# Cross-attention with a new order inside its steps: maxima, scores, maxima, weighting, values, keys

## What is computed

```python
q1 = x1 @ Wq1                      # x1 = layernorm(x), 8 heads of 64
k  = concatenate([x1 @ Wk1, x2 @ Wk2], axis=1)   # x2 = context, 256 + 4096 keys
v  = concatenate([x1 @ Wv1, x2 @ Wv2], axis=1)
sim  = einsum('bihd,bjhd->bhij', q1, k) * scale
attn = softmax(sim, axis=-1)
out  = einsum('bhij,bjhd->bihd', attn, v) @ Wo + bo
```

## Time and profile before

| | us |
|---|---|
| three runs | 1909.60, 1912.25, 1913.94 (median 1912.25) |
| the profiled execution, its own time | 1913.26 |
| its span, first to last instruction | 1911.5 |
| PE busy | 1654.2 (87%) |
| DVE busy | 1221.1 (64%) |
| ACT busy | 727.5 (38%) |
| POOL busy | 424.3 (22%) |

### The profile page before, as it was taken

How to read it: one execution, slowest core, us unless ns; L and a number is a source line. 1 busy time by engine, 2 the same in 40 slices (tenths; PEclk the granted TensorE clock), 3 DMA queues, 4 the chain that set the end, 5 groups by cost and what they waited for, 6 DMA issues and landing times. The chain is left out here.

```text
span 1911.5 us, 30641 instructions
## 1 busy us (share of the span) xinstructions
PE 1654.2 (87%) x12438; PEld 1266.1 (66%) x12438; DVE 1221.1 (64%) x1434; ACT 727.5 (38%) x970; POOL 424.3 (22%) x254
## 2 busy tenths in 40 slices
PE   5999989999989999989999997287357776999999
PEld 4777767777767777767777775165133334788888
DVE  4686586586586576586576585634579994644444
ACT  3444354344354334344334333122353331334332
POOL 4200041000041000041000000110056661445552
PEclk9999999999999999999999999597579998799999
DMA  4000120000120000120000000100000001111100
GB/s 151 12 18 1 45 73 1 12 18 1 37 81 1 12 18 1 35 81 4 12 10 10 1 1 4 54 1 0 15 0 1 1 0 34 67 56 44 55 11 23
DMA packets 43357, 47.89 MB, mean 25 GB/s; under 512 B 5200, under 2 KB 30672, under 8 KB 43232
## 3 DMA queue, kind: packets, MB, share of 16 engines
q1 hardware_dynamic: 43232, 46.07, 7.8%
HBM read 45.02 MB, written 1.05 MB: 24 GB/s over the span
## 5 line engine op out<-in xcount | busy, mean ns | idle before, releaser
L493 DVE TENSOR_REDUCE xa_maxes<-psum 128x2 f32<-128x1024 f32 (+1 forms) x288 | 332.5, 1162 | 267.3 <-PE psum L674 267.3
L419 ACT ACTIVATE xa_probs<-psum 128x1024 f32<-128x1024 f32 x272 | 269.0, 1026 | 323.9 <-PE psum L707 311.1
L514 DVE TENSOR_TENSOR xa_prob_sum<-xa_prob_sum,xa_probs 128x1024 f32<-128x1024 f32 x240 | 308.9, 1287 | 11.2 <-ACT xa_probs L419 10.4
L719 PE MATMUL psum<-xa_probs,xa_vals 128*64 128x256 f32 x2176 | 263.1, 385 | 2.1 <-DVE xa_heads_T L528 1.6
L719 PEld LDWEIGHTS psum<-xa_probs,xa_vals 128*64 128x64 f32 x2176 | 146.5, 136 | 93.0 <-issue 23.9
L344 POOL TENSOR_TENSOR xa_w_lo<-xa_stage,xa_w_hi 128x768 fp32r<-128x768 f32 x16 | 31.9, 1994 | 617.0 <-ACT xa_w_hi L379 617.0
L606 PE MATMUL psum<-xa_wv_hi,xa_ctx_hi 128*128 128x256 f32 x512 | 148.9, 291 | 21.3 <-DVE xa_maxes L493 18.6
L701 PE MATMUL psum<-xa_q_hi,xa_k_hi 64*128 64x256 f32 x1088 | 156.5, 284 | 0.6 <-issue 0.6
L705 PE MATMUL psum<-xa_q_hi,xa_k_lo 64*128 64x256 f32 x1088 | 154.6, 280 | 0.0
L707 PE MATMUL psum<-xa_neg_max,xa_ones 64*128 64x256 f32 x1088 | 154.5, 280 | 0.0
L703 PE MATMUL psum<-xa_q_lo,xa_k_hi 64*128 64x256 f32 x1088 | 154.0, 279 | 0.0
(11 more groups left out here) (273 smaller groups left out, 3482.8 us busy)
## 6 DMA issues: line engine op xcount, KB each, us to landing
xa_ctx_in<-in_ctxT_dram SPq DMA_DIRECT2D x32, 512.0 KB, 3.7
xa_stage<-in_L_xattn_Wk_dram SPq DMA_DIRECT2D x32, 128.0 KB, 2.3
xa_stage<-in_L_xattn_Wv_dram SPq DMA_DIRECT2D x16, 256.0 KB, 3.0
ex_raw<-in_L_ffn_w_gate_dram SPq DMA_DIRECT2D x8, 512.0 KB, 3.6
ex_raw<-in_L_ffn_w_up_dram SPq DMA_DIRECT2D x8, 512.0 KB, 4.5
ex_raw<-in_L_ffn_w_down_dram SPq DMA_DIRECT2D x8, 512.0 KB, 3.5
xa_stage<-in_L_xattn_Wq_dram SPq DMA_DIRECT2D x16, 128.0 KB, 2.3
X<-in_x_dram SPq DMA_DIRECT2D x1, 1024.0 KB, 5.4
```

The lines of the kernel that those rows point to most:

```text
L419: nc.scalar.activation(probs[:, n % RING, :], S[:, 2 * (n % 2):2 * (n % 2) + 2, :].rearrange("p h q -> p (h q)"), ACT.Exp, scale=HD ** -0. ...
L493: dve.tensor_reduce(maxes[:, qt, :, g:g + 1], max_banks(v, g, qt)[:, :, 0:group_keys(g)[1]], AX_X, ALU.max).then_inc(max_reduced, 1)
L514: dve.tensor_tensor(prob_sum[:, :], prob_sum[:, :], probs[:, n % RING, :], ALU.add).then_inc(summed, 1)
L719: i = pe.matmul(O[half[h], 0:N1], vals[:, 2 * j + t, lanes:lanes + HD], probs[:, n % RING, (2 * h + t) * N1:(2 * h + t + 1) * N1], start=( ...
```

## The change

In a step PE does the weighting directly behind the first half of the maxima, then the values, then (in step 2 of some units) the output projection, then the keys. ACT's queue follows: it stores the values before the high part of the keys. In the last step PE scores the second half of the maxima before the first, which `turn` tells DVE, and turns the maxima before the values; the second tile of values waits there until DVE has read the turned maxima. Sums of a unit are inverted and applied at the end of DVE's step 0, no longer in step 1. DVE's queue in a step becomes reduction of (d - 1, tile 1), low part of the keys of group d, a sum, reduction of (d, tile 0), a sum. No instruction is added or taken away.

```diff
+        def turn(v, g, qt):
+            return 1 - qt if v > 0 and g == NG - 1 else qt
@@ ScalarE
+                for c, j in v_due(u, d):
+                    store_values(c, j)
                 if d + 1 < NG and v < U:
                     store_k_hi(v, d + 1)
-                for c, j in v_due(u, d):
-                    store_values(c, j)
@@ VectorE
             def reduce_max(v, g, qt):
-                dve.wait_ge(max_scored, (v * NG + g) * QT + qt + 1)
+                dve.wait_ge(max_scored, (v * NG + g) * QT + turn(v, g, qt) + 1)
...
                         reduce_max(v, 0, 0)
-                        split_keys(v, 1)
-                    add_probs(u, 1)
+                    if u > 0:
+                        invert_sums(u - 1)
+                        normalize(u - 1)
                     continue
                 if v < U:
                     reduce_max(v, d - 1, 1)
-                if d == 1 and u > 0:
-                    invert_sums(u - 1)
-                    normalize(u - 1)
-                if d >= 2 and not (d == STEPS - 1 and v < U):
-                    add_probs(u, 2 * d - 1)
-                if v < U:
-                    reduce_max(v, d, 0)
-                if d == 2 and u > 0 and u % PAIRS == 0:
-                    add_output(u // PAIRS - 1)
+                    if d < STEPS - 1:
+                        split_keys(v, d)
+                    else:
+                        reduce_max(v, d, 1)
+                        reduce_max(v, d, 0)
+                        reduce_rows(v)
+                        split_keys(v, d)
+                        store_neg_max(v)
+                add_probs(u, 2 * d - 1)
                 if d < STEPS - 1:
+                    if v < U:
+                        reduce_max(v, d, 0)
+                    if d == 2 and u > 0 and u % PAIRS == 0:
+                        add_output(u // PAIRS - 1)
                     add_probs(u, 2 * d)
-                    if v < U:
-                        split_keys(v, d + 1)
                     if d == 4 and u % PAIRS == 2 and u + 2 < U:
                         split_own(u // PAIRS + 1)
-                elif v < U:
-                    reduce_max(v, d, 1)
-                    reduce_rows(v)
-                    add_probs(u, 2 * d - 1)
-                    store_neg_max(v)
@@ TensorE
                 if following:
-                    score_for_max(v, d, 0, values)
-                    maxima = (v * NG + d) * QT + 1
                     if d == STEPS - 1:
                         score_for_max(v, d, 1, values)
-                    if d == 2 and u > 0 and u % PAIRS == 0:
-                        project_output(u // PAIRS - 1)
-                    if d + 1 < NG:
-                        project_keys(v, d + 1, maxima, values)
-                    for c, j in v_due(u, d):
-                        project_values(c, j, maxima)
-                        values += 1
+                    score_for_max(v, d, 0, values)
+                    maxima = (v * NG + d) * QT + (2 if d == STEPS - 1 else 1)
                 if d == 0 and u > 0:
                     sum_probs(u - 1)
                 for j in step_tiles(d - 1):
                     weigh(u, j)
                 if d == STEPS - 1:
                     weigh(u, HG - 1)
-                    if following:
+                if following:
+                    if d == STEPS - 1:
                         turn_maxima(v, values)
+                    for c, j in v_due(u, d):
+                        if d == STEPS - 1 and j % 2 == 1:
+                            pe.wait_ge(neg_max_ready, v + 1)
+                        project_values(c, j, maxima)
+                        values += 1
+                    if d == 2 and u > 0 and u % PAIRS == 0:
+                        project_output(u // PAIRS - 1)
+                    if d + 1 < NG:
+                        project_keys(v, d + 1, maxima, values)
```

## The result

| | before | after |
|---|---|---|
| median of the runs, us | 1913.10 | 1940.24 |
| ratio (95% interval) | | 1.0148 (1.0134 to 1.0162) |
| span of the profiled execution, us | 1911.5 | 1936.6 |

The changed kernel is 27 us slower. The direction and its main cause were forecast; the size was 18.4 us, and 1940.24 lies just above the range that ended at 1940. The profiled execution of the changed kernel was the quickest of its four (1938.28), so the profiles differ by 25.1 us and the medians by 27.1.

The account below looks back on a forecast made before the run. PE, busy 87%, was taken as the bound, with some 46 us of waits. Terms -10.4 + 7 + 11.6 + 3.2 + 2 - 4 + 9 = +18.4 on 1912.25 gave 1931 us, range 1919 to 1940.

Parts of the forecast that it names:

- The weights come late: Last step of 7 odd units: next queries wait 3.5 us for the weights' low half; 1.65 each, +11.6 us.
- The clock: Half clock behind new idle stretches: 8 falls in 10 at 1.5 us, 0.6 for own latents; +9 us, between 0 and 15.
- Steps with values: Steps 3 to 7 of odd units, 35 times: values' wait for the reduction grows from 0.23 to about 0.4; +7 us.
- Step 1 of the even units: 7 times: the values' 1.48 us wait for a reduction behind the previous unit's inversion and normalization goes; -10.4 us.
- The own latents: Units 2, 6, 10: DVE's split of own latents starts later, delaying maxima by 1.05 us each; +3.2 us, between 0 and 6.
- The switches: Changes of PE tile shape: 0.02 us more in each of 105 steps; +2 us, between -5 and +6.
- the small terms: Heads' wait, DVE before step 2, last maxima and three old weights' waits (each growing 0.45); together -4 us, between -6 and +1.
- the weights were not hidden: Rival at the start of even units: POOL's low half of the weights ready when values end; 1898 us, chance 0.07.
- The cases that it calls slower: Forecast 0.72, clock staying up (1922) 0.12, nothing won in step 1 of even units (1941) 0.04; given as 0.87.

Follow-up runs that it names:

- experiment 1: Changed kernel, but ACT makes the weights' high half before storing the two value tiles in the odd units' last step; 1898.39 us, ratio 0.9931.
- experiment 4: Kernel before, with the two value tiles moved behind the turned maxima in the odd units' last step; 1930.69 us, ratio 1.0117.
- Experiment 3: Changed kernel plus 14 matmuls nobody reads at the start of even units, where PE waits for the weights; 1923.63 us, ratio 1.0067.
- Experiment 6: Kernel of experiment 1, with DVE's second reduction of maxima before the first sum in each step but the last; 1877.12 us, ratio 0.9817.
- Experiment 5: Kernel before, with the previous unit's sums summed, inverted and applied early in step 0; 1910.90 us, ratio 0.9996.
- experiment 10: Kernel before, with weights split before the context chunk in the last step and own latents split in two halves, steps 5 and 6; 1904.47 us, ratio 0.9957.

## Why the prediction was wrong, step by step

The two profiles can be compared place by place, each step measured from its first score to the first score of the next, and summed over all units:

| place | forecast, us | by the profiles, us |
|---|---|---|
| last step of the odd units and the queries behind it, 7 | 11.6 + 8.4 = 20.0 | 22.7 |
| step 1 of the even units, 7 | -10.4 | -11.7 |
| steps 3 to 7 of the odd units, 35 | 7 | 4.2 |
| the own latents, 3 | 3.2 + 0.6 = 3.8 | 9.9 |
| everything else | 2 - 4 = -2 | -0.1 |
| sum | 18.4 | 25.0 |

**The weights come late: right.** 3.27 us of chain in front of the queries and 3.5 of idle time were forecast, 3.30 of idle time stand in the row. +1.65 for each unit was forecast, 10.05 - 8.45 = 1.60 was measured, 11.2 instead of 11.6 us. Experiments 1 and 4 show the cause from both sides.

**The clock: mis-sized, and this is the step that failed.** "At half clock 3.4 us do the work of 1.7, so a fall costs up to 1.7; I take 1.5. [...] I take 8 falls in 10: 7 x 0.8 x 1.5 = 8.4, and 0.6 for the longer waits of units 2, 6 and 10: **+9**, between 0 and 15." How often the clock falls was about right, 6 times in 7. What a fall costs was not: four of the six lasted 6.8 us, twice as long as in the one row from which the price was taken. Against unit 7, where the clock stayed up, the two falls of 3.4 us cost 1.5 each, as taken, and the four of 6.8 cost 2.6 each, 13.4 together. The waits of the own latents were given 0.6; the clock fell behind all three, and that is 5.7 us more than before. Over the whole of cross-attention the half clock grew by 41 us, which can cost up to 20.4, where 15 was the bound. Experiment 3 supports the size: with the seven waits filled, the half clock went back from 58 to 17 us and the time fell by 16.6. In experiment 4, behind waits of the same 3.3 us, all seven falls lasted 3.4 us, the length that the prediction had taken. What makes a fall last 6.8 us in one order and 3.4 in the other stays open.

**Steps with values: right in mechanism, too high.** A wait of about 0.4 was forecast, 0.39 stands in the row, and the step is 9.32 - 9.21 = 0.11 longer, not 0.2 (the values may start a little earlier on the clock of weighting). All 35 together are 4.2 us longer instead of 7. Step 2 of these units, taken as unchanged, is 0.6 to 0.7 us longer in units 3, 7 and 11 and 0.1 shorter in the others. Experiment 6 took this wait away and won 21 us, since the whole wait goes, not only its growth.

**Step 1 of the even units: right, with a reason that was too simple.** The steps are 7 x 1.67 = 11.7 us shorter. Experiment 5 shows that the inversion's move alone wins nothing.

**The own latents: right in place, too low.** 1.05 more for each was forecast, 3.69 - 2.3 = 1.4 was measured, 4.2 us instead of 3.2; the other 5.7 of the 9.9 are the clock's. `own_lo` starts later, and it also lasts 2.83 us instead of 2.27, as it meets POOL's instruction earlier; that second part was not priced.

**The switches and the small terms: too low together.** -2 was forecast, and near 0 came. A step without values takes 6.02 us in both orders, so the +2 for the switches was 0. The three old waits for the weights of 2.8 us didn't grow by 0.45 each: two shrank to 2.2, the third grew to 3.3. Against that stand short new waits, which make steps 4 and 5 of the even units (in units 2, 6 and 10 also 6 and 7) 4.9 us longer in sum. What stands there is read from the traces and was not tested: in step 4 of all seven even units with values' weights to split, a sum on DVE now starts earlier in POOL's instruction and lasts 2.91 us, where it lasted 1.62 to 1.65 before. In unit 2:

```profile
243.39 2.91 DVE L518 TENSOR_TENSOR xa_prob_sum<-xa_prob_sum,xa_probs 128x1024 f32<-128x1024 f32 x1
```

I had not priced such meetings.

Two sums of the prediction are off by themselves. The cases that it calls slower add up to 0.88, not 0.87; and with its own bounds for clock and switches the range would have run from 1914.7 to 1940.7, not from 1919 to 1940.

The rivals: the weights were not hidden, but what it would be worth was forecast well; with the weights hidden (experiment 1) the change gives 1898.39, and 1898 was forecast for that case. Part of that is luck: by its profile the steps with values are 2.9 us cheaper and the own latents 4.8 dearer than forecast.

## What to carry to other kernels

When work is moved on the busiest engine, look for the chains that it used to cover on engines that are nearly idle: here ACT was busy 37% and POOL 22%, and a chain of three short instructions had 0.06 us to spare. With its cover moved away the kernel was 42 us slower than with the same order and the chain repaired. Then look at the order within the queue of the idle engine; one instruction in front of another repaired it. An idle stretch of the busiest engine has to be priced with the clock behind it: seven stretches of 3.3 us cost 23 us of idle time and about 13 us of half clock.

## What the runs showed of the hardware

**DVE and POOL take turns.** A sum of two tiles in SBUF takes DVE 1.22 us. One that starts while POOL subtracts two tiles in SBUF ends 1.08 us after POOL's instruction ends, whenever it had started. DVE, in the changed kernel:

```profile
289.39 3.35 DVE L514 TENSOR_TENSOR xa_prob_sum<-xa_probs 128x1024 f32<-128x1024 f32 x1
```

POOL at the same time:

```profile
289.27 2.38 POOL L343 TENSOR_TENSOR xa_ctx_lo<-xa_ctx_in,xa_ctx_hi 128x1024 fp32r<-128x1024 f32 x1 [8.22 <-ACT xa_ctx_hi L396]
```

It ends at 292.74, and POOL's ended at 291.65: 1.08 or 1.09 in all of the 29 such meetings of the kernel before, and in nearly all of the 28 of the changed kernel. Read so, it isn't slowed by a share, but stands still until POOL is done and then does all of its own work: the remainder is 1.08 us for 1024 elements a partition, 0.55 for the 512 of `own_lo` and 0.28 for the 256 of its half. So half the work takes little less time when most of the time is POOL's (experiment 10), and 1.22 us became 3.35 where the meeting began early. It goes the other way too: POOL's subtraction of 1024 elements, 2.38 us alone, ends 2.25 us after a sum in which it had started, and so lasted 3.38 at 245.18 us of the changed kernel. The Trainium skill (Advanced Engine Details and Errata, GPSIMD Details) says that the Pool engine shares a read and a write interface with DVE and conflicts with DVE instructions that have two SBUF inputs; the traces agree and give it this form. DVE's instructions with an input in PSUM are not held up: in the kernel before, 5 low parts of keys (one input in PSUM, one in SBUF) and 27 reductions of maxima (one input, in PSUM) lie wholly inside an instruction of POOL and take 0.68 and 1.21 to 1.23 us, as elsewhere. Seven reductions of the collected maxima (one input, in SBUF) inside POOL's instructions take 0.19 us, like the nine outside.

**The length of an idle stretch doesn't tell how long the half clock behind it lasts.** Behind PE's waits of 2.8 us in the kernel before it was 0.50 for 3.4 us or not at all. Behind the seven new waits of 3.3 us in the changed kernel it was 0.50 for 6.8 us four times, for 3.4 twice and once not at all; behind the seven waits of 3.3 us in experiment 4 it was 0.50 for 3.4 us each time. Filled with matmuls that nobody reads, the waits of the changed kernel were cheaper by 16.6 us (experiment 3).
